# Local attention: the values' product behind q and k, keys turned ahead of the odd probabilities; delta stage: scores, rates, a power, two norms and one gate in other slots

## What is computed

```python
# delta rule, per head, over time (keys 96 wide, values 192)
q, k, v = (silu(conv4(h @ W)) for W in (Wq, Wk, Wv)); q, k = l2norm(q) * scale, l2norm(k)
S = S * exp(g_t); delta = (v_t - k_t @ S) * b_t; S = S + outer(k_t, delta); o_t = q_t @ S
o = rmsnorm(o) * silu(h @ Wg)
# local attention, 8 heads of 64, a window looks at itself and the one before
q = l2norm(q) * qs; k = l2norm(k) * ksc; q, k = rotary_xpos(q, k)
out = softmax(mask(q @ k.T * 8)) @ v; x = x + out @ wo
```

## Time and profile before

| what | value |
|---|---|
| median of 3 runs | 3595.34 us (3591.72 to 3601.11) |
| the profiled execution's own time | 3593.64 us |
| its span | 3591.9 us |
| busy share PE, DVE, ACT, POOL | 90%, 74%, 57%, 50% |
| delta stage with its preparation | about the first 1500 us |
| local attention, four passes | beginning at 1621, 2017, 2797 and 3191 us |

### The profile page before, as it was taken

How to read it: one execution, slowest core, us unless ns; L and a number is a source line. 1 busy time by engine, 2 the same in 40 slices (tenths; PEclk the granted TensorE clock), 3 DMA queues, 4 the chain that set the end, 5 groups by cost and what they waited for, 6 DMA issues and landing times. The chain is left out here.

```text
span 3591.9 us, 86970 instructions
## 1 busy us (share of the span) xinstructions
PE 3217.1 (90%) x32714; PEld 2426.5 (68%) x32714; DVE 2675.9 (74%) x5718; ACT 2061.6 (57%) x4823; POOL 1796.2 (50%) x1631
## 2 busy tenths in 40 slices
PE   4899999999999999798999999987988799899998
PEld 3678888788788888655666566655665466656665
DVE  5677777777777777477777677776999577767775
ACT  3566666666666666325765477623443466536662
POOL 3355555555555555235664366622222566436662
PEclk9699999999999999999999999997999899999999
DMA  4111111111111110142222212231221122222132
GB/s 130 25 27 27 27 26 27 27 29 27 28 28 37 30 26 13 32 121 54 49 70 68 67 46 52 69 97 46 72 63 41 47 53 69 64 72 48 47 75 74
DMA packets 406989, 182.42 MB, mean 51 GB/s; under 512 B 233552, under 2 KB 381744, under 8 KB 404016
## 3 DMA queue, kind: packets, MB, share of 16 engines
q1 hardware_dynamic: 406576, 176.87, 20.1%
HBM read 94.20 MB, written 40.12 MB: 37 GB/s over the span
## 5 line engine op out<-in xcount | busy, mean ns | idle before, releaser
L1205 POOL TENSOR_TENSOR delta_cv<-delta_cv,delta_last_tap 96x256 f32<-96x256 f32 (+1 forms) x384 | 331.8, 864 | 557.0 <-DVE delta_cv L1646 557.0
L1985 POOL TENSOR_TENSOR g_a_rn<-g_a_clip,held_minus_half 128x16 f32<-128x16 f32 x64 | 186.3, 2911 | 240.7 <-DVE g_a_clip L2250 240.7
L1985 POOL TENSOR_TENSOR f_a_rn<-f_a_clip,held_minus_half 128x16 f32<-128x16 f32 x64 | 186.3, 2910 | 237.9 <-DVE f_a_clip L2250 209.7
L2202 ACT ACTIVATE g_a_pr<-g_ps,g_a_nb,g_a_rn 128x128 f32<-128x128 f32 x512 | 185.5, 468 | 125.4 <-DVE g_a_nb L2284 125.4
L2202 ACT ACTIVATE f_a_pr<-f_ps,f_a_nb,f_a_rn 128x128 f32<-128x128 f32 x512 | 185.5, 468 | 124.8 <-DVE f_a_nb L2284 124.8
L1474 ACT ACTIVATE delta_cv<-delta_ps,delta_conv_qk 96x256 f32<-96x256 f32 x256 | 121.4, 474 | 229.6 <-PE delta_ps L1299 228.5
L1638 DVE SCALAR_TENSOR_TENSOR delta_cv<-delta_ps,delta_conv_qk,delta_cv 96x256 f32<-96x256 f32 x256 | 122.1, 477 | 170.8 <-ACT delta_last_tap L1476 168.8
L1243 PE MATMUL delta_ps<-delta_state,delta_qk 96*128 96x192 f32 x1024 | 197.4, 336 | 27.1 <-issue 26.5
L1243 PEld LDWEIGHTS delta_ps<-delta_state,delta_qk 96*128 96x128 f32 x1024 | 164.5, 191 | 37.2 <-issue 33.8
L1988 POOL TENSOR_TENSOR f_a_rot_c<-f_a_rot_c,f_a_rot_s 128x1024 f32<-128x1024 f32 x64 | 150.5, 2351 | 0.0
L1988 POOL TENSOR_TENSOR g_a_rot_c<-g_a_rot_c,g_a_rot_s 128x1024 f32<-128x1024 f32 x64 | 150.4, 2350 | 0.0
(11 more groups left out here) (349 smaller groups left out, 10288.5 us busy)
## 6 DMA issues: line engine op xcount, KB each, us to landing
f_a_vm<-f_a_v SPq DMA_DIRECT2D x128, 130.0 KB, 2.3
g_a_vm<-g_a_v SPq DMA_DIRECT2D x128, 130.0 KB, 2.3
delta_gd<-delta_dram_row SPq DMA_DIRECT2D x16, 1024.0 KB, 4.9
window_vm<-window_v SPq DMA_DIRECT2D x64, 128.0 KB, 2.3
f_m_x<-y SPq DMA_DIRECT2D x24, 256.0 KB, 3.5
delta_dram_inv<-delta_sub SPq DMA_DIRECT2D x16, 256.0 KB, 2.1
f_m_more<-x SPq DMA_DIRECT2D x16, 256.0 KB, 4.1
held_table<-const_rotation SPq DMA_DIRECT2D x4, 1024.0 KB, 6.7
```

The lines of the kernel that those rows point to most:

```text
L1205: pool.tensor_tensor(cv[0:M, t % 3], cv[0:M, t % 3], last_tap[0:M, t % 3], ALU.add).then_inc(summed.sem, 1)
L1985: pool.tensor_tensor(rn[:, u % 2], clip[:, u % 2], minus_half[:], ALU.pow).then_inc(rn_sb.sem, 1)
L2202: e = act.activation(pr[:, u % 2, half, i, :], ps[:, score_bank(u, half), i * P:(i + 1) * P], ACT.Exp, bias=nb[:, u % 2, half, i:i + 1], s ...
```

## The change

In the delta stage (line numbers of the kernel before): the second half's scores move from slots 18 and 19 to slots 21 and 22 (`KQ_AT`). The rates (L1695 to L1700) move from slot 19 to 20, and the one of them that needs the power of the norms (L1704, bvr) moves to slot 17. bm on POOL moves from slot 22 to 21. For the first chunk of each unit the power L1229 moves from slot 21 to 22 and the two products L1236 from slots 21 and 22 to 23 and 24; those of the second chunk stay. On ACT the gate's silu of slot 22 is taken ahead of `light`. SP's load of the next unit's decays, which follows the scores, moves from slot 20 to 23.

In local attention: PE projects the values right behind queries and keys and turns the keys ahead of the odd probabilities; ACT squares k before it copies turned q; DVE sums the squares before it copies the odd probabilities.

```diff
-    KK_AT, KQ_AT = ((6, 7), (9, 10)), ((13, 14), (18, 19))
+    KK_AT, KQ_AT = ((6, 7), (9, 10)), ((13, 14), (21, 22))
+    POWER_AT, NORMED_AT = (16, 15), (17, 15)
...
-                n = unit(t, K_NORM + 8)
+                n = unit(t, K_NORM + 7)
...
-                C = chunk(t, 15)
-                if C is not None:
-                    ostat_sb.need(pool, C)
...
-                    C = chunk(t, 15 + i)
...
+                for cc in range(2):
+                    C = chunk_of(t, POWER_AT[cc], cc)
                     if C is not None:
+                        ostat_sb.need(pool, C)
+                        o_normed.need(pool, C - 1)
+                        pool.tensor_tensor(of[:], ostat[:, 1, :], minus_half[:, 0:H], ALU.pow).then_inc(of_sb.sem, 1)
+                    for i in range(2):
+                        C = chunk_of(t, NORMED_AT[cc] + i, cc)
...
-            def misc(t):
+            def gates(t, ahead):
                 for cc in range(2):
                     for k, when in enumerate(GATE_AT[cc]):
                         C = chunk_of(t, when, cc)
-                        if C is not None:
+                        if C is not None and ahead == (k == 0 and cc == 1):
...
                 products_of(t)
+                gates(t, True)
                 if t > 0:
                     light(t - 1)
+                gates(t, False)
                 misc(t)
...
-                n = unit(t, K_NORM + 5)
+                n = unit(t, K_NORM + 6)
...
+                n = unit(t, K_NORM + 3)
+                if n is not None:
+                    p = n % 2
                     rn_sb.need(dve, n)
                     dve.tensor_tensor(bvr[:, p], rn[:, p], ex[:, BETA, 2 * n:2 * n + 2, :].rearrange("p t h -> p (t h)"),
...
             if 0 < u < TILES:
                 project_qk(pe, u)
+                project_v(pe, u)
             if within(i):
                 transpose_p(i, 0)
-            if 0 < u < TILES:
-                project_v(pe, u)
             if within(i + 1):
                 transpose_q(i + 1)
+                transpose_k(i + 1)
             if within(i):
                 transpose_p(i, 1)
-            if within(i + 1):
-                transpose_k(i + 1)
...
                 copy_v(u)
+                square(u, 1)
             if within(i + 1):
                 copy_qt(i + 1)
-            if within(u):
-                square(u, 1)
...
+            if 0 < u < TILES:
+                squared_norms(dve, u)
             if within(i):
                 copy_pt(i)
-            if 0 < u < TILES:
-                squared_norms(dve, u)
```

More of the change, by code:

```diff
@@ L1224, in _ @@
                         pool.tensor_tensor(mine, mine, gate[:, HB * i * DV:HB * (i + 1) * DV], ALU.mult).then_inc(o_gated.sem, 1)
-                C = chunk(t, 15)
-                if C is not None:
-                    ostat_sb.need(pool, C)
-                    o_normed.need(pool, C - 1)
-                    pool.tensor_tensor(of[:], ostat[:, 1, :], minus_half[:, 0:H], ALU.pow).then_inc(of_sb.sem, 1)
-                for i in range(2):
-                    C = chunk(t, 15 + i)
-                    if C is not None:
[L1233 to L1237, removed]
+                for cc in range(2):
+                    C = chunk_of(t, POWER_AT[cc], cc)
+                    if C is not None:
+                        ostat_sb.need(pool, C)
[3 more added lines that the diff above has]
+                        C = chunk_of(t, NORMED_AT[cc] + i, cc)
+                        if C is not None:
+                            of_sb.need(pool, C)
+                            o_gated.need(pool, C)
+                            mine = o[:, cc, HB * i:HB * i + HB, :]
+                            pool.tensor_tensor(mine, mine, of[:, HB * i:HB * i + HB].unsqueeze(2).to_broadcast([P, HB, DV]), ALU.mult)\
+                                .then_inc(o_normed.sem, 1)
         @block.tensor
@@ L1503, in misc @@
                             emptied(act.activation(gate[:, k * 512:(k + 1) * 512], ps[:, bank, :], ACT.Silu), ("gate", C, k))
+            def misc(t):
                 for cc in range(2):
```

## The result

The changed kernel takes **3634.73 us** (median of four runs, 3633.45 to 3639.3), the kernel before beside it 3597.54 us: a ratio of 1.0107, 95% interval 1.009 to 1.0125. It is about 38 us slower. The forecast was 3623 us.

What follows compares the result with a forecast made beforehand. The prediction took PE as the fullest engine, so its idle time counts. Local attention -51, new order +12, held-up rates +30 and clock +38 sum to +29 on 3593.6, giving 3623 us; range 3545 to 3650, 8 in 10.

Steps and rivals of the forecast that it cites:

- the likeliest case: Whole kernel: rates held up in the delta stage and PE at the lower clock, 3623 us, range 3600 to 3650, chance 0.45.
- Local attention, -51: Local attention: mask 0.43 us earlier per step (46 us) and 5 us at pass starts, together -51 us, bounds -35 and -60.
- POOL is hidden and stays so: Local attention: summing squares earlier on DVE starts POOL's power 0.6 us earlier, but POOL stays hidden.
- The new order alone, +12: Delta stage: the gate of slot 22 waits for the scores' bank, 0.8 us later per unit, 15 times, +12 us.
- The rates held up, +30: Delta stage, slot 20: POOL's operations make DVE's rates end 2.0 us late, 15 times, +30 us.
- the clock, +38: Delta stage: PE idles 3.9 us ahead of slot 22's gate, then the lower clock costs 2.5 us, 15 times, +38 us.
- Which operations hold them up: Delta stage, slot 20: the first or second rate waits for POOL's multiplication until 897.44, the next for its addition until 898.12.
- a rival with 0.05: Delta stage: rates held up by three POOL operations instead of two, +57 us instead of +30, lower clock, 3650 us; chance 0.05.
- The rival on the other side: Delta stage, slot 20: rates not held up, clock mostly holds, 3555 to 3565 us, more likely 3545 if stalls go; chance 0.33.
- The clock holds: Delta stage: PE's idle stretch is broken up or shorter, no clock loss, -51 + 12 + 30 = -9, 3585 us; chance 0.17.

Runs made afterwards that it cites:

- run 1: Only the local attention's edits on PE, ACT and DVE, put on the kernel before: 3544.12 us, ratio 0.9851 to the kernel before.
- runs 7 and 8: The kernel before with the attention's new order on PE alone (3611.56 us), and with those on PE and ACT but not DVE's (3611.57 us).
- run 3: The changed kernel with the rates brk, nbrk and npb back in slot 19: 3554.93 us, ratio 0.9877 to the kernel before.
- run 6: The changed kernel with five products of 240 columns that nobody reads, on PE ahead of slot 22's gate: 3598.44 us, ratio 1.0012 to the kernel before.
- run 5: The changed kernel, rates still in slot 20, with POOL's multiplication of output by gate one slot later: 3629.28 us, ratio 1.0103 to the kernel before.

## Why the prediction came out as it did

The result lies in the likeliest case, 12 us above its 3623 and within its own range of 3600 to 3650. Term by term:

- **Local attention, -51.** Measured -54 (run 1). The step's 0.43 us is 9.57 - 9.15 = 0.42. Right in size. One sentence of its reasons was wrong: "POOL is hidden and stays so". POOL's scaling is what PE waits for as soon as DVE's edit is left out (runs 7 and 8); the edit on DVE was costed at nothing, and without it the gain is gone.
- **The new order alone, +12.** Measured +9 (run 3 against run 1; 0 to 18 by the intervals), the difference of 27 us lost by the scores' slots and some 17 won by the rest. Within it the wait ahead of ks is 1.6 us, not 2.6; ahead of a projection behind it stand another 0.55. The gate waits for the bank that it shares with the scores, as worked out, but 1.1 us and not 1.9.
- **The rates held up, +30, and the clock, +38**, together 68. Measured 83 together (changed kernel against run 3). The rows of run 6 divide it: over 14 units the changed kernel takes 76.9 us more than run 3, of which 39.4 are the same 10808 products of PE at a clock of 0.95 instead of 0.99, and 37.5 are waiting. Over 15 units that is some 42 and 40: both terms have the right mechanism, the clock nearly its size (2.8 us a unit, not 2.5), the hold-up a third too small (2.7, not 2.0). The rates themselves account for 2.2 of the 2.7; the other 0.5 isn't followed further.
- **Which operations hold them up.** The rates were to end with the addition ("the first or second waits until 897.44, the next until 898.12"): three of 15 units do, the one shown among them. In seven npb is held up by the next multiplication too, which as a rule for all units was a rival with 0.05; in five npb gets by. That the average came out near 2.0 is in part luck: it is the middle of a spread from 0.6 to 3.5 us, by what npb meets and how early brk comes.
- **The rival on the other side** ("were DVE 0.7 us earlier, it would win") named the right condition: with the rates freed the kernel takes 3555 us, its forecast 3545 to 3565. It was given 0.33. In none of the 15 units of the changed kernel do the rates get by freely. With the multiplication a slot later they don't either, since DVE and POOL are let go by the same tap (run 5). Whether DVE, 0.7 us earlier in the changed kernel, would win was not run.
- **"The clock holds", 3585 us**: run 6 holds it at the gate and takes 3598: the hold-up is more than the 30 that this rival reckons with.

## What to carry to other kernels

Before tiny operations are moved to another slot, look at what the engine that shares their way to SBUF starts at that moment, and at who releases it: if the same instruction lets both go, they meet in every round (run 5), and an operation of 0.2 us can cost as much as the one beside it, here up to 1.85 us. A wait of 0.3 us that ends a chain often has others right behind it; edits that shorten one chain each may be worth nothing in part and 54 us together, so take a change apart before you throw it away. And where one half of a change gains and the other loses, measure the halves: here the simplest of the fastest kernels was the gaining half with a single table of four numbers from the other.

## What was not expected of the hardware

- A small DVE operation that meets POOL's multiplication or addition lasts until that one operation ends, then gets through, and the next of DVE's meets the next of POOL's: 0.21, 1.74 and 0.77 us in a row, where beside POOL's short steps they take 0.16 to 0.27 (run 3). All of these operations of DVE have 16 columns. When both start together, either may come first: npb, which starts within 0.02 us of an operation of POOL in each of 15 units, is held up in ten and gets by in five. The Trainium skill (SBUF — State Buffer, Who interferes with whom) says the same of a DVE instruction with two SBUF inputs and of some with one; these rows agree. But the shift of 0.17 us inside POOL's power of 2.91 us is not held up in the changed kernel either (0.17 us in all 16 between 2960 and 3098 us), and there the page's rule goes too far: for that operation of POOL the row decides.
- An idle stretch of 3.64 us ahead of the gate is followed by half the clock for 6.8 us; in 14 units together PE's products take 39 us longer than in run 3. With waits of at most 1.7 us in the stage (run 3) the clock stayed at 0.99.
